# Order of the attention inside a unit of the first block: logits, softmax and low parts

## The reference

```python
B, Q, S1, S2 = (4, 32, 256, 256)
D, H, K, F = (256, 16, 128, 1024)
...
def _cross_attention(q_in, kv_in, wq, bq, wk, bk, wv, bv, wo, bo, bias_k, bias_v):
    qh = (q_in @ wq + bq).reshape(b, q_len, H, K)
    kh = (kv_in @ wk + bk).reshape(b, t, H, K)
    vh = (kv_in @ wv + bv).reshape(b, t, H, K)
    kh = jnp.concatenate([kh, jnp.broadcast_to(bias_k, (b, 1, H, K))], axis=1)
    vh = jnp.concatenate([vh, jnp.broadcast_to(bias_v, (b, 1, H, K))], axis=1)
    logits = jnp.einsum('bqhk,bthk->bhqt', qh, kh) / scale
    weights = jax.nn.softmax(logits, axis=-1)
    ctx = jnp.einsum('bhqt,bthk->bqhk', weights, vh).reshape(b, q_len, H * K)
    return ctx @ wo + bo
...
h = _layer_norm(x, ln1_scale, ln1_offset)
x = res + _cross_attention(h, xf_1, wq1, ...)
res = x
h = _layer_norm(x, ln2_scale, ln2_offset)
x = res + _cross_attention(h, xf_2, wq2, ...)
h = _layer_norm(x, ln_mlp_scale, ln_mlp_offset)
h = jax.nn.gelu(h @ w_fc1 + b_fc1, approximate=False) @ w_fc2 + b_fc2
```

## Time and profile before

| | |
|---|---|
| median of three runs | 1475.01 us |
| the profiled execution's own time | 1475.47 us |
| its span, first to last instruction | 1473.7 us |
| TensorE matmul busy | 1411.5 us, 96% |
| TensorE weight load busy | 1263.8 us, 86% |
| VectorE busy | 899.7 us, 61% |
| ScalarE busy | 627.8 us, 43% |
| GpSimd busy | 340.8 us, 23% |
| mean granted TensorE clock | 0.977 of full |

### The profile page before, as it was taken

One profiled execution on the slowest core, in us unless ns is written; L12 is line 12 of the kernel. 1 busy time (PEld: TensorE's weight loads), 2 busy tenths in 40 slices (PEclk: granted clock), 3 DMA queues, 4 the chain that ended last, 5 costly groups with the idle time before them and its releaser, 6 DMA issues. The chain is left out here.

```text
span 1473.7 us, 28434 instructions
## 1 busy us (share of the span) xinstructions
PE 1411.5 (96%) x11575; PEld 1263.8 (86%) x11575; DVE 899.7 (61%) x1929; ACT 627.8 (43%) x1055; POOL 340.8 (23%) x322
## 2 busy tenths in 40 slices
PE   4999999999999999999999999997998999997898
PEld 3899998989998889999999999885887888887787
DVE  6566757666666676766666666664522477776322
ACT  4534333433333664333434334353323246665521
POOL 4201101101011111110101101101853045555654
PEclk8999999999999999999999999995999999998899
DMA  5000000000000000100100000000000000001000
GB/s 174 30 30 2 29 4 27 29 2 29 30 1 30 2 30 1 30 30 1 30 29 1 30 26 5 30 1 25 2 0 8 1 1 0 0 0 62 4 29 28
DMA packets 28984, 30.26 MB, mean 21 GB/s; under 512 B 651, under 2 KB 28883, under 8 KB 28883
## 3 DMA queue, kind: packets, MB, share of 16 engines
q1 hardware_dynamic: 28658, 28.72, 6.2%
q10 hardware_dynamic: 226, 0.10, 0.0%
HBM read 26.72 MB, written 2.10 MB: 20 GB/s over the span
## 5 line engine op out<-in xcount | busy, mean ns | idle before, releaser
L286 POOL TENSOR_TENSOR WLO<-W,WHI 128x512 fp32r<-128x512 f32 x68 | 85.6, 1293 | 754.0 <-DVE WHI L613 754.0
L167 PE MATMUL bank<-SRC_HI,WHI 128*128 128x512 f32 (+1 forms) x576 | 229.9, 399 | 3.9 <-PEq L248 3.9
L168 PE MATMUL bank<-SRC_LO,WHI 128*128 128x512 f32 (+1 forms) x576 | 229.2, 398 | 0.0
L169 PE MATMUL bank<-SRC_HI,WLO 128*128 128x512 f32 (+1 forms) x576 | 229.0, 398 | 0.0
L558 DVE STREAM_TRANSPOSE PRT<-PR 32x256 f32<-32x256 f32 x512 | 223.3, 436 | 8.4
L465 ACT ACTIVATE QT<-bank,PB 128x512 f32<-128x512 f32 x128 | 88.3, 690 | 194.7 <-PE bank L169 194.7
L581 DVE TENSOR_TENSOR CLO<-bank,CHI 128x512 fp32r<-128x512 f32 x128 | 87.8, 691 | 136.6 <-ACT CHI L489 136.5
L167 PE MATMUL bank<-WHI,CHI 128*128 128x256 f32 x512 | 153.9, 301 | 0.8 <-DVE CLO L581 0.8
L167 PE MATMUL bank<-WHI,SRC_HI 128*128 128x256 f32 x512 | 149.5, 292 | 0.0
L169 PE MATMUL bank<-WHI,CLO 128*128 128x256 f32 x512 | 144.5, 282 | 0.0
L168 PE MATMUL bank<-WLO,CHI 128*128 128x256 f32 x512 | 144.5, 282 | 0.0
(11 more groups left out here) (182 smaller groups left out, 2976.9 us busy)
## 6 DMA issues: line engine op xcount, KB each, us to landing
W<-in_wall SPq DMA_DIRECT2D x18, 1024.0 KB, 5.5
V<-in_ctx SPq DMA_DIRECT2D x4, 512.0 KB, 5.3
X<-in_x SPq DMA_DIRECT2D x4, 512.0 KB, 6.4
mlp_w<-in_w SPq DMA_DIRECT2D x2, 1024.0 KB, 8.2
out<-X SPq DMA_DIRECT2D x4, 512.0 KB, 2.9
W<-in_qw SPq DMA_DIRECT2D x1, 256.0 KB, 4.0
W<-in_kw SPq DMA_DIRECT2D x1, 256.0 KB, 4.3
W<-in_vw SPq DMA_DIRECT2D x1, 256.0 KB, 6.3
```

The lines of the kernel that those rows point to most:

```text
L167: e.matmul(dst, a_hi, b_hi, start=start, stop=False, **kw)
L168: e.matmul(dst, a_hi, b_lo, start=False, stop=False, **kw)
L169: return e.matmul(dst, a_lo, b_hi, start=False, stop=stop, **kw)
L286: i = e.tensor_tensor(WLO[a][:, j, :, :], W[a][:, j, :, :], WHI[a][:, j, :, :].bitcast(F32), ALU.subtract)
```

## The change

Three moves inside `slot`, and nothing else. No instruction is added or taken out.

- TensorE: the logits of unit n, with their waits and the small product for g = 0, are issued behind `values(0)` (and behind the bridge transposes) and ahead of P times V of unit n-1. Before, they stood behind `values(1)`.
- ScalarE: the exp of unit n stands behind the high parts and ahead of `values_out(1)`; before, behind it.
- VectorE: maximum and difference of unit n (and the addition L594) stand ahead of the low parts of unit n-1; before, behind them.

```diff
@@ TensorE
                                 i.then_inc(bw_turned, 1)
+                        if front:
+                            e.wait_ge(q_out, 2 * n + 2)
+                            e.wait_ge(k_out, 2 * n + 2)
+                            e.wait_ge(kb_set, n + 1)
+                            if back:
+                                e.wait_ge(sub_done, n)
+                            if g == 0:
...
+                                i.then_inc(bw_done, 1)
+                            for h in range(2):
+                                for q in range(GTOK // S):
+                                    p, b = q // 2, q % 2
+                                    i = e.matmul(logits[b * S:(b + 1) * S, h, p * KEYS:(p + 1) * KEYS],
+                                                 QT[:, h, q * S:(q + 1) * S], KT[:, h, q, :], start=True, stop=True)
+                            i.then_inc(s_done, 1)
                         if back:
                             e.wait_ge(v_out, 2 * n)
                             e.wait_ge(pt_out, n)
                             e.wait_ge(x_settled, 2 * n)
...
                             e.wait_ge(k_out, 2 * n + 2)
                             norm_turn(e, norm, *norm_now, PROJ[2:])
-                        if front:
...
@@ ScalarE
                         if front:
+                            e.wait_ge(sub_done, n + 1)
+                            e.activation(ex[:, :, :], sub[:, :, :], ACT.Exp, scale=SCALE).then_inc(exp_done, 1)
+                        if front:
                             values_out(1)
                         if n == 0:
                             e.wait_ge(cur_set, norm_now[0] + 1)
                             norm_scale(e, norm, *norm_now, PROJ[2:])
-                        if front:
-                            e.wait_ge(sub_done, n + 1)
-                            e.activation(ex[:, :, :], sub[:, :, :], ACT.Exp, scale=SCALE).then_inc(exp_done, 1)
@@ VectorE
                             round_set(pair + 1, 1 - a)
-                        if back:
-                            for h in range(2):
-                                e.wait_ge(c_hi, 2 * n - 1 + h)
-                                e.tensor_tensor(CLO[:, h, :], bank[3 + h][:, :], CHI[:, h, :].bitcast(F32),
-                                                ALU.subtract).then_inc(c_lo, 1)
-                        if norm_now is not None and not front:
...
                         if front:
                             e.wait_ge(s_done, n + 1)
...
                                             .to_broadcast([P, 2, GT, KEYS]), ALU.subtract).then_inc(sub_done, 1)
+                        if back:
+                            for h in range(2):
+                                e.wait_ge(c_hi, 2 * n - 1 + h)
+                                e.tensor_tensor(CLO[:, h, :], bank[3 + h][:, :], CHI[:, h, :].bitcast(F32),
+                                                ALU.subtract).then_inc(c_lo, 1)
+                        if norm_now is not None and not front:
...
```

More of the change, by code:

```diff
@@ L362, in slot @@
                                 i.then_inc(bw_turned, 1)
-                        if back:
-                            e.wait_ge(v_out, 2 * n)
-                            e.wait_ge(pt_out, n)
-                            e.wait_ge(x_settled, 2 * n)
-                            for h in range(2):
[L369 to L373, removed]
-                        if front:
[L375 to L379, removed]
                         if front:
@@ L400, in slot @@
                             i.then_inc(s_done, 1)
+                        if back:
+                            e.wait_ge(v_out, 2 * n)
+                            e.wait_ge(pt_out, n)
+                            e.wait_ge(x_settled, 2 * n)
+                            for h in range(2):
+                                for p in range(GT):
+                                    i = e.matmul(bank[3 + h][:, p * P:(p + 1) * P],
+                                                 V[(n - 1) % 2][:, p, h * K:(h + 1) * K],
+                                                 PRT[:, h * GT + p, :], start=True, stop=True)
+                                i.then_inc(c_done, 1)
+                        if front:
+                            values(1)
+                        if n == 0:
+                            e.wait_ge(k_out, 2 * n + 2)
+                            norm_turn(e, norm, *norm_now, PROJ[2:])
                         if norm_now is not None and back and front:
@@ L602, in slot @@
                                             .to_broadcast([P, 2, GT, KEYS]), ALU.subtract).then_inc(sub_done, 1)
+                        if back:
[4 more added lines that the diff above has]
+                        if norm_now is not None and not front:
+                            e.wait_ge(x_settled, 2 * n)
+                            norm_stats(e, norm, *norm_now)
+                            norm_rstd(e, norm, *norm_now)
+                            norm_apply(e, norm, *norm_now)
                         if back:
```

## The result

The changed kernel's four runs took 1497.77, 1497.99, 1503.90 and 1506.63 us, median 1500.95, against 1474.38 of the kernel before (four runs): 1.0182 times as long, 95% interval 1.0166 to 1.0197. Its runs lie further apart than those of before, which stay within 2.6 us, and the longer ones have the lower mean clock: 0.977 for the two short ones, 0.973 and 0.970 for the others. The direction was forecast; the size was not: 1492.5 was said, with 1500 as the upper end.

What follows compares the result with a forecast made beforehand. TensorE's own work was taken to set the pace (matmuls over 96% of the span). Regular slots +10.1, late-VectorE slots +7.8 and gaining slots -0.7 made +17.2 us on 1475.47, forecast as 1492.5, own range 1484 to 1497, full range 1479 to 1500.

Steps and rivals of the forecast that it cites:

- the cover of the low parts: Regular slots: only `values(1)` is left over the 3.30 us chain from P times V to the second low part; +0.19 each.
- The earlier exp: ScalarE, regular slots: the earlier exp buys nothing, since VectorE's sum over it starts later, behind the two additions to X.
- A: Rival, regular slots: `values(1)` covers the chain, -0.05 us each, while norm and bridge slots still pay 7.8; 1479.4 us; chance 0.10.
- B: Rival, all slots: TensorE's switches set every slot and low parts none, so it is faster, 1471.5 us; chance 0.05.
- D: Rival, VectorE in regular slots: the first low part is late by 0.1 to 0.2 us, about 1500 us; chance 0.08.
- how far P times V moves: TensorE, regular slots: P times V starts 1.16 us later with its first weight load not hidden, 1.22 in all.
- The forecast's upper end: Regular slots: P times V behind the logits pays 0.22 us instead of about 0.16, giving +0.25 a slot.
- The longer chain: Regular slots: from the start of P times V to the end of the second low part, put at 3.30 us.
- a slot without a wait: Regular slot if nothing waits: the output projection's second product 4.56 us after P times V's old start, that is -0.05.
- C, the clock falls in the new gaps: Rival, slots 30, 31, 62, 63: TensorE's clock at 0.50 through the output projection, +20 us, 1513 us; chance 0.03.
- the norm and bridge slots: Slots 29 to 33 and 61 to 63, where VectorE is late: waits for the low parts sum to +7.8 us.
- 10.1 - 0.7: 53 regular slots at +0.19 us give +10.1; stalls of P times V vanishing in slots 1 and 34 give -0.7.

Runs made afterwards that it cites:

- run 1: The changed kernel with VectorE's old order (both low parts ahead of maximum and difference) back in every slot: 1487.74 us (1.0088).
- run 6: The kernel before with all three moves everywhere except slots 29 to 33 and 61 to 63: 1487.83 us (1.0092).
- run 7: The changed kernel with the output projection's wait split by heads, the second head's low part awaited only ahead of its first product: 1478.68 us (1.0024).
- run 5: The kernel before with all three moves in slots 29 to 33 and 61 to 63 only: 1487.31 us (1.0090).
- run 3: The kernel before with ScalarE's move alone (exp ahead of `values_out(1)`): 1476.97 us, one execution.
- run 4: The kernel before with VectorE's move alone (maximum and difference ahead of the low parts): 1749.92 us, one execution.
- run 8: The changed kernel with the output projection's wait split by heads and VectorE's old order in slots 29 to 33 and 61 to 63: 1473.91 us (1.0007).
- run 9: The kernel before with all three moves in slot 0, and VectorE's softmax ahead of the additions to X in slots 30 to 33, 62, 63: 1469.54 us (0.9963).
- run 10: As run 9, with ScalarE's square root of a norm ahead of `values_out(0)` and the early softmax also in slots 29 and 61: 1467.09 us (0.9953).
- run 11: As run 10, with the output projection's wait split by heads in every slot: 1463.12 us (0.9923).
- run 2: The kernel before with one edit, TensorE's logits between P times V and `values(1)`: 1478.34 us (1.0024).

## Why the prediction was right, and where it was not

**Right: the mechanism and both places.** The logits ran early; the cover of the low parts fell from 4.39 to 3.33 us; the output projection waited in each regular slot; the norm slots waited 1.2 us because maximum and difference stand ahead of the low parts. Runs 1 and 6 show the regular slots' loss apart from the norm slots', run 7 that it is the wait, and run 5 the norm slots' loss. The earlier exp bought nothing (run 3). Rivals A and B are out: no regular slot hides the chain (least +0.20). D is out: the first low part starts when its high part is there, and run 1, with VectorE's old order, has the same +0.248.

**Wrong size: the term "how far P times V moves".** It took 0.06 us for the bare weight load at P times V; 0.10 was measured (2.05 against 1.95 us). The forecast's upper end let P times V pay the same 0.22 as the output projection's first product, which gives +0.25; I took the smaller value, by the rows of a load behind a stall. The longer chain, 3.41 instead of 3.30, is that same 0.10: +0.25 a slot instead of +0.19, 3.1 us over 53 slots. By the same 0.10 a slot without a wait comes out at 4.60, not 4.56, and run 7 measured +0.006 where the forecast had -0.05.

**Wrong: "C, the clock falls in the new gaps", put at 0.03 and so at nothing in the sum.** The argument against it was one row: slot 33 of before waits 0.84 us in a stretch at full clock. The new waits are 1.0 and 2.1 us as TensorE's matmuls see them, and with them the clock does fall: in the profiled run twice, for 10.2 and 3.4 us, worth 6.1 us; in the runs of 1503.90 and 1506.63 us the lower mean clock says that it fell for longer, where is not known, since only one execution is profiled. I had also priced C as falls in all four slots or none, which is neither. By the medians, the norm and bridge slots cost 12.6 us (run 5) where 7.8 were forecast, and the rest 13.2 (run 6) where 10.1 - 0.7 = 9.4 were. The median left the range by 0.95 us; either miss alone would have left it inside. The profiled execution, 1497.99, is inside only because its start and end were 3.0 us shorter than those of before, which nothing in the forecast stands for: that part is luck.

**Open.** What decides in one execution whether slot 30's wait is followed by a fall and slot 31's is not. The link to the waits is shown (runs 4 and 5 have the waits and falls; the profiled executions of runs 1, 3, 6 and 8 to 11 have neither the new waits in these slots nor a fall between slots 1 and 63), a rule is not: run 7's wait of 1.53 us in slot 33 had no fall. The 3.5 us of run 2 in slots 0 and 1 were read from one execution. And what scatters run 8 is not known.

## What to carry to other kernels

Before moving an instruction ahead on a saturated engine, list for each handover what lay between producer and consumer and subtract the moved piece: here 1.06 us of cover went to save nothing that was late. A wait on TensorE is priced twice, as the wait and the weight load it lays bare, and where it is as long as the 1.0 and 2.1 us here a third time, as a chance of half clock behind it. If several producers feed one consumer, let the consumer wait for each where it first needs it: that took back the whole loss of the regular slots and about half of that of the norm slots (run 7), and in a slot without cover it was worth 4 us, most of it by a clock that stayed up (run 11).

## What the runs showed of the hardware

The clock of TensorE fell to 0.50 some 2 us after a wait of about 1 us had ended, with the engine fully busy in between (wait up to 494.32, fall at 496.4), and it stayed there 10.2 us. The same wait in slots 31, 62 and 63 had no fall behind it. In run 7 neither the waits of 0.44 us in slots 30, 31, 62 and 63 nor that of 1.53 in slot 33 had one. In run 5 the clock fell at the end of slot 33's wait of 2.13 us and stayed at 0.50 for 3.4 us. Run 4, with a wait of 2.7 us or more in each regular slot, kept the full clock from 500 to 560 us and was at 0.88 from 400 to 460.

A weight load behind a semaphore wait was not started ahead of it: 0.22 us from the output projection's first product to its second, where 0.12 is the spacing. Behind the logits' matmuls with a stationary operand of 64 columns the next load was bare as well: 0.21 instead of 0.11 us from the first to the second matmul of P times V.
